# Local attention with values product in channel-major form, tile by tile in turn, and weights divided on GpSimd; state-space stage with rests and root kept in PSUM

## The chip, the cores and the metric

The kernel runs on one core of a Trainium2 chip. A core has TensorE (called PE in the profile; its weight loads are the row PEld), VectorE (DVE), ScalarE (ACT), GpSimd (POOL), SyncE (SP, which issues DMAs here) and 16 DMA engines. The engines run side by side and meet through semaphores. SBUF is the on-chip memory; PSUM holds TensorE's results in eight banks of 128 partitions by 512 fp32 words. The metric is the device time of one execution in microseconds, less is better.

## The reference, cut to what matters

Eight sequences of 256 tokens with 128 channels pass through an attention layer, a hard-routed feed-forward layer, a state-space layer and six layers of windowed local attention, each with a gated feed-forward layer. The change touches the last two of these four stages.

```python
# state-space stage: the norm in front of it, and the low-rank projection
h = _layernorm(x) * (1 + ca) + sa
x_dbl = xs @ W_x                    # 64 columns for dt, 16 for B, 16 for C
# local attention, 6 layers, 16 heads of 64 channels, windows of 32 tokens
q, k = rotary(l2norm(q)*qs), rotary(l2norm(k)*ksc)
sim = einsum('bhwie,bhwje->bhwij', bq, bk2) * QK_SCALE   # bk2: own window and the one before
attn = softmax(where(mask, -max, sim))
out = einsum('bhwij,bhwje->bhwie', attn, bv2)
x = out.reshape(b, n, INNER) @ Wo + x
# feed-forward layer
xn = (x - mu) / sqrt(var + 1e-05) * g + bln
x = (a * gelu(gate)) @ W2 + b2 + x                        # a, gate = split(xn @ W1 + b1)
```

## The kernel before, in words

The program has four stages: attention, routed layer, state-space (`mamba1`) and local attention (`local1`). The data that the change touches is fp32; an fp32 matmul appears in the trace as two passes, a transpose as one.

`local1` is a software pipeline. A step is one sequence (of 8) of one layer (of 6), so there are 48 steps, and the loop runs 50 iterations. In iteration `it` three parts run together: FRONT works on step `it`, MID on step m = it-1, LATE on step n = it-2. Each engine has a hand-written order (`body` in each engine's block) of the same pieces, and each engine works strictly through its own. The table `order` gives every PSUM result ("job") a bank; `jobs.filled` and `jobs.taken` are semaphore waits for "written" and "copied out", and `jobs.free` is the wait before a bank is written again.

The names of the jobs: Z are projections of tokens to queries and keys (`project`, L2052; first digit is the half of the tokens t, second is query 0 or key 1), T their transposes (`turn`, L2063), S scores (`scores`, a mask matmul at L2073 and 64 small ones at L2080), V values of the tokens (`project_values`, L2093), P transposed softmax weights (`turn_weights`, L2105), O the product of weights and values (`values`, L2120), OT its transposes (`turn_outputs`, L2135), WO the output projection (`outputs`, L2146), mean and var the norm, F the hidden layer (`hidden`, L2172), OUT2 its second matmul (`hidden_out`, L2181).

In `values` the stationary operand is a 64 by 32 piece of the transposed weights `pT` and the moving operand 64 columns of values. The result O has tokens on partitions. VectorE divides it by the row sums on the way out (`by_sum`, L2496, into `Ot`), TensorE turns `Ot` (OT), and ScalarE copies that to `oT` (`take_outputs`, L2298), which WO reads. GpSimd has `take_tokens` (L2395), `rotary_sum` (L2402) and `unit` (L2412). VectorE has `less_maximum` (scores minus maximum into z), ScalarE `exps` (L2268), VectorE `sums` (row sums and reciprocal).

The values are needed twice, for two window alignments (`Vo`, `Ve`). ScalarE copies V out of PSUM into `Vo` (`take_values`, L2278), signals `V_ready` and `wv_used`, and SyncE then copies `Vo` to `Ve` by four DMAs (`share_values`, L2001 and L2002). SyncE has one order for everything, `layer` in its block, and the weights of the next layer pass through it too:

```python
if b == NB - 1 and not last:
    sp.wait_ge(qk_used, l * NB + NB)
    load_front(there)
    sp.wait_ge(wv_used, l * NB + NB)
    load_values(there)
share_values(l * NB + b)                 # waits for V_ready of this step
if b == 1 and not first:
    ...load_hidden(here)...load_late(here)
    rest_loaded(l)                       # sem_inc(mid_ok), sem_inc(late_ok)
if b == NB - 1 and not last:
    front_loaded(l + 1)                  # sem_inc(front_ok), sem_inc(values_ok)
```

TensorE waits for `front_ok` at the head of the iteration, before Z00, and for `mid_ok` at the head of `outputs` (WO).

`mamba1` is a pipeline over the eight sequences. `root_variance` writes the reciprocal root of the variance to `lrs` in SBUF and VectorE's `by_root` (L1725) multiplies by it. `first_rest` and `second_rest` (L1729, L1734) form what is left of an fp32 number after its bf16 parts, in `rest` in SBUF.

Of the kernel before, what the change touches and what calls it, by code (L numbers as in the profile page):

```python
# [14 lines left out]
NT = T // 128  # L15
# [1357 lines left out]
def mamba1(core):  # L1373
    nc, d = core.nc, core.dram
    NG = NS // 2
    with ExitStack() as ctx:
# [23 lines left out]
        xd_ready, p1_ready, p2_ready, r2_ready, parts_ready, soft_ready, dt_ready = (  # L1400
            S(n, 1) for n in ("xdbl", "part1", "part2", "rest2", "parts", "soft", "dt"))
# [10 lines left out]

        made = lambda b, name: b + part_of[name]
# [13 lines left out]
        with nc.Block() as block:  # L1427
# [158 lines left out]
            def _(act):  # L1586
# [28 lines left out]
                def root_variance(it):  # L1615
                    act.wait_ge(*jobs.filled(it, "var"))
                    nc.scalar.activation(lrs[:, :], jobs.out("var")[:, 0:T], ACT.Ln, bias=core.eps[:, EPS_LN:EPS_LN + 1])\
                        .then_inc(jobs.sem_drained("var"), 1)
                    act.drain()
                    nc.scalar.activation(lrs[:, :], lrs[:, :], ACT.Exp, scale=-0.5).then_inc(scaled.sem, 1)  # L1620
# [20 lines left out]
                def second_part(it, parts):  # L1641
                    act.wait_ge(*jobs.taken(it, "XD"))
                    nc.scalar.activation(parts[32:64, :], rest[:, :], ACT.Copy).then_inc(p2_ready.sem, 1)

                def third_part(it, parts):
                    act.wait_ge(r2_ready.sem, r2_ready.at(it, 1))
                    nc.scalar.activation(parts[64:96, :], rest[:, :], ACT.Copy).then_inc(parts_ready.sem, 1)
# [62 lines left out]
            def _(dve):  # L1710
# [12 lines left out]
                def by_root(it):  # L1723
                    dve.wait_ge(scaled.sem, scaled.at(it, 1))
                    nc.vector.tensor_tensor(cent[:, :], cent[:, :], lrs[:, :], ALU.mult).then_inc(hm_ready.sem, 1)  # L1725

                def first_rest(it, parts):
                    dve.wait_ge(p1_ready.sem, p1_ready.at(it, 1))
                    nc.vector.tensor_tensor(rest[:, :], jobs.out("XD")[DTR:96, 0:T], parts[0:32, :], ALU.subtract)\  # L1729
                        .then_inc(jobs.sem_drained("XD"), 1)  # L1730

                def second_rest(it, parts):
                    dve.wait_ge(p2_ready.sem, p2_ready.at(it, 1))
                    nc.vector.tensor_tensor(rest[:, :], rest[:, :], parts[32:64, :], ALU.subtract).then_inc(r2_ready.sem, 1)  # L1734
# [91 lines left out]
def local1(core):  # L1826
# [3 lines left out]
    with ExitStack() as ctx:  # L1830
# [22 lines left out]
        Ot = sb("Ot3", [128, NT, H1, E1])  # L1853
# [21 lines left out]
        with nc.Block() as block:  # L1875
# [29 lines left out]
            def _(dve):  # L1905
# [4 lines left out]
                with dve.Fori(0, NB) as b:  # L1910
# [26 lines left out]
        e_ready = S("exps", NT)  # L1937
# [4 lines left out]
        order = (two(FRONT, "Z00", 7, 2) + two(MID, "T11", 5, 3) + [(LATE, "WO", 4)] + two(MID, "T10", 1, 6)  # L1942
                 + two(FRONT, "Z01", 0, 5) + [(LATE, "mean", 4)] + two(MID, "P0", 7, 2) + two(MID, "S1", 6, 1)
                 + two(FRONT, "T00", 3, 7) + [(LATE, "var", 2)] + two(FRONT, "Z11", 0, 4) + two(MID, "O0", 3, 5)
                 + [(FRONT, "V0", 2), (FRONT, "V1", 7)] + two(FRONT, "Z10", 1, 6) + two(MID, "P1", 2, 3)
                 + [(LATE, "F0", 7), (LATE, "F1", 0), (LATE, "F2", 5)] + two(MID, "O1", 4, 2)
                 + [(FRONT, "V2", 3), (FRONT, "V3", 6)] + two(FRONT, "T01", 7, 1) + [(LATE, "OUT2", 5)]
                 + two(MID, "OT1", 3, 2) + two(FRONT, "S0", 0, 6) + two(MID, "OT0", 1, 4))
# [14 lines left out]
        with nc.Block() as block:  # L1963
# [74 lines left out]
            def _(pe):  # L2038
# [27 lines left out]
                def scores(it, t):  # L2066

                    for j in range(2):
                        pe.wait_ge(*jobs.taken(it, f"T{t}{1 - t}.{j}"))
# [38 lines left out]
                def values(it, m, t):  # L2108
# [6 lines left out]
                    for i in range(H1):  # L2115
                        j, h = i % 2, i // 2
                        p, n = 64 * j, f"O{t}.{j}"
                        for w in range(4):
                            V = Ve if w % 2 == 0 else Vo
# [3 lines left out]
                        if i >= H1 - 2:  # L2123
                            last.then_inc(jobs.sem_filled(n), 1)

                def turn_outputs(it, t):

                    for j in range(2):
                        pe.wait_ge(*jobs.taken(it, f"O{t}.{j}"))
                    for j in range(2):  # L2130
                        n = f"OT{t}.{j}"
                        pe.wait_ge(*jobs.free(it, n))
                        for i in range(4):
                            pair = Ot[:, t, 8 * j + 2 * i:8 * j + 2 * i + 2, :].rearrange("p s e -> p (s e)")
                            last = nc.tensor.transpose(jobs.out(n)[:, i * 128:(i + 1) * 128], pair, core.ident[:, :])  # L2135
                        last.then_inc(jobs.sem_filled(n), 1)

                def outputs(it, n):

                    pe.wait_ge(mid_ok, n + 1)  # L2140
                    for t in range(NT):
                        for j in range(2):
                            pe.wait_ge(*jobs.taken(it - 1, f"OT{t}.{j}"))
# [41 lines left out]
                def body(it, front, mid, late):  # L2185
# [13 lines left out]
                    do(mid, pair("T11"), turn, m, 1, 1)  # L2199
# [540 lines left out]
```

## Time and profile before

| what | value |
|---|---|
| time, median of 3 runs | 2901.34 us (2898.34 to 2903.61) |
| the profiled execution | 2920.77 us, its span 2919.0 us |
| PE busy | 2534.2 us (87%) |
| DVE busy | 2114.7 us (72%) |
| ACT busy | 1789.1 us (61%) |
| POOL busy | 1299.7 us (45%) |
| local attention, about | 1250 to 2880 us of the span |
| state-space, about | 850 to 1204 us |

Busy time is a sum over instructions that may overlap on PE, so what a piece costs TensorE is better read from start to start in the timeline. The profile's chain of waits that ended last shows only the last copies and says nothing here, so the stages are read by windows and by the timeline of one iteration. An idle time in brackets stands before the instruction of that row, and the name behind the arrow is what ended it.

### The profile page before, as it was taken

The page shows a single profiled execution, that of the slowest core. Times are in us where ns is not written, and L with a number is a line of the kernel's source. Part 1 is how long each engine was busy: PE and PEld are TensorE (multiplying, and loading weights), DVE is VectorE, ACT ScalarE, POOL GpSimd, SP SyncE. Part 2 cuts the span into 40 slices and gives each one's busy share as a digit, 9 for nine tenths or more (in the row PEclk, how much of TensorE's full clock was granted, in tenths as well). Part 3 has the DMA queues.
Part 4 walks back from the last instruction along what each step waited for, and adds up shares of the span by engine and source line. Part 5 has one row for each costly group of instructions (what it writes and reads, how often), then busy time and mean ns, then how long its engine had stood idle before and what let it go on. Part 6 is the DMA issues. An engine that isn't in the chain of part 4 may idle for free. (4 is left out here: it accounts for less than half of the span.)

```text
span 2919.0 us, 95512 instructions
## 1 busy us (share of the span) xinstructions
PE 2534.2 (87%) x35932; PEld 1738.5 (60%) x35932; DVE 2114.7 (72%) x3264; ACT 1789.1 (61%) x3671; POOL 1299.7 (45%) x966
## 2 busy tenths in 40 slices
PE   7999758885737777569999999999999999999995
PEld 4777446664523334226777677776777767776774
DVE  5888543213217999558888888888888888888883
ACT  4666513332216677346777777777777777777772
POOL 2444232223023444335555555555555555555550
PEclk9999968987858999779999999999999999999997
DMA  9000016860420000011121112111211111121110
GB/s 331 24 0 0 4 41 175 227 168 22 130 65 1 0 0 0 16 50 27 31 53 40 25 25 59 40 25 25 54 45 25 47 40 29 34 54 33 25 36 18
DMA packets 124766, 149.22 MB, mean 51 GB/s; under 512 B 12016, under 2 KB 111536, under 8 KB 120240
## 3 DMA queue, kind: packets, MB, share of 16 engines
q1 hardware_dynamic: 120592, 139.81, 18.0%
q0 software_dynamic: 4096, 8.40, 1.0%
q8 instruction: 45, 0.74, 0.1%
q14 instruction: 33, 0.27, 0.0%
HBM read 76.86 MB, written 27.26 MB: 36 GB/s over the span
## 5 line engine op out<-in xcount | busy, mean ns | idle before, releaser
L2402 POOL TENSOR_TENSOR c<-a,bq 128x1024 f32<-128x1024 f32 x192 | 454.2, 2366 | 380.5 <-DVE bq L2458 380.5
L2412 POOL TENSOR_TENSOR qn<-c,ss 128x1024 f32<-128x1024 f32 x192 | 378.4, 1971 | 28.5 <-issue 7.2
L2052 PE MATMUL ps<-wqk,xs 128*128 128x512 f32 x768 | 373.0, 609 | 12.2 <-POOL xs L2395 8.7
L2237 ACT ACTIVATE sq<-ps 128x512 f32<-128x512 f32 x384 | 223.4, 594 | 93.3 <-PE ps L2052 93.2
L2457 DVE TENSOR_TENSOR a<-ps,tab 128x512 f32<-128x512 f32 x384 | 262.8, 684 | 24.1 <-ACT sq L2237 13.7
L2458 DVE TENSOR_TENSOR bq<-ps,tab 128x512 f32<-128x512 f32 x384 | 261.6, 681 | 0.0
L2465 DVE TENSOR_REDUCE ss<-sq 128x16 f32<-128x1024 f32 x192 | 232.4, 1211 | 14.5 <-issue 14.5
L1458 POOL TENSOR_TENSOR hC<-hs,Cs 128x1024 f32<-128x1024 f32 x64 | 151.9, 2376 | 199.9 <-ACT Cs L1609 104.5
L2052 PEld LDWEIGHTS ps<-wqk,xs 128*128 128x128 f32 x768 | 135.9, 192 | 150.1 <-issue 138.4
L2063 PEld LDWEIGHTS ps<-ident,qn 128*128 128x128 f32 x1536 | 172.2, 141 | 79.4 <-issue 66.9
L2063 PE MATMUL ps<-ident,qn 128*128 128x128 f32 x1536 | 204.8, 276 | 3.2 <-PEq L2045 3.2
L2093 PE MATMUL ps<-wv,xs 128*64 128x512 f32 x768 | 187.7, 609 | 3.2 <-PEq L2045 3.2
L2146 PE MATMUL ps<-oT,wo 128*128 128x256 f32 x768 | 176.8, 384 | 1.8 <-PEq L2045 1.8
L2254 ACT ACTIVATE qT<-ps 128x512 f32<-128x512 f32 x192 | 104.3, 595 | 95.8 <-PE ps L2063 95.8
L2120 PEld LDWEIGHTS ps<-Ve,pT 64*32 64x32 f32 x6144 | 125.7, 105 | 56.0 <-issue 56.0
L1757 DVE TENSOR_TENSOR_SCAN hs<-dA,ps 128x1024 f32<-128x1024 f32 x64 | 146.4, 2287 | 14.6 <-issue 13.9
L1532 PE MATMUL ps<-hC,ident 128*128 128x512 f32 x256 | 139.8, 685 | 19.3 <-POOL hC L1458 19.1
L2146 PEld LDWEIGHTS ps<-oT,wo 128*128 128x128 f32 x768 | 144.3, 193 | 20.2 <-issue 2.0
L2278 ACT ACTIVATE Vo<-ps 128x512 f32<-128x512 f32 x192 | 114.8, 598 | 62.9 <-PE ps L2093 58.6
L2080 PEld LDWEIGHTS ps<-kT,qT 64*32 64x32 f32 x12288 | 127.3, 105 | 43.3 <-issue 43.3
L2496 DVE TENSOR_TENSOR Ot<-ps,sm 128x512 f32<-128x512 f32 x192 | 123.7, 686 | 31.6 <-PE ps L2120 21.0
L2080 PE MATMUL ps<-kT,qT 64*32 64x64 f32 x12288 | 143.0, 225 | 2.5 <-issue 2.5
(309 smaller groups left out, 5882.3 us busy)
## 6 DMA issues: line engine op xcount, KB each, us to landing
Ve<-Vo SPq DMA_DIRECT2D x96, 256.0 KB, 4.3
Ve<-Vo SPq DMA_DIRECT2D x96, 192.0 KB, 4.4
win_rows<-rows_q SPq DMA_DIRECT2D x24, 256.0 KB
outs_q<-win_out SPq DMA_DIRECT2D x24, 256.0 KB
wqk<-in_wqkv SPq DMA_DIRECT2D x6, 1024.0 KB, 5.0
leaves<-in_f_w SPq DMA_DIRECT2D x9, 576.0 KB
leaves<-in_q_w SPq DMA_DIRECT2D x1, 4608.0 KB, 18.8
leaves<-in_k_w SPq DMA_DIRECT2D x1, 4608.0 KB, 22.3
```

What stands on the lines that cost most here:

```text
L1458: nc.gpsimd.tensor_tensor(four(hC), four(hs), spread(Cs[:, s, :], 2), ALU.mult).then_inc(hC_ready.sem, 1)
L2052: nc.tensor.matmul(jobs.out(n), xs[:, t * 128:(t + 1) * 128], wqk[:, (2 * y + s) * 512:(2 * y + s + 1) * 512], start=True, stop=True).then ...
L2063: last = nc.tensor.transpose(jobs.out(n)[:, i * 128:(i + 1) * 128], src, core.ident[:, :])
L2080: last = nc.tensor.matmul(jobs.out(n)[w * W:(w + 1) * W, m * 64:(m + 1) * 64], qT[p:p + 64, t, m, w * W:(w + 1) * W], kT[p:p + 64, even:od ...
L2093: last = nc.tensor.matmul(jobs.out(n)[p:p + 64, :], xs[:, g * 64:(g + 1) * 64], wv[:, p * 8:p * 8 + 512], start=True, stop=True, tile_posi ...
L2146: last = nc.tensor.matmul(jobs.out("WO")[:, 0:T], wo[:, i, :], oT[:, i, :], start=(i == 0), stop=(i == H1 // 2 - 1))
L2237: nc.scalar.activation(sq[:, y, :, s, :], heads_view(jobs.out(n)), ACT.Square).then_inc(sq_ready.sem, 1)
L2402: nc.gpsimd.tensor_tensor(f(c), f(a), f(bq), ALU.add).then_inc(c_ready.sem, 1)
L2412: nc.gpsimd.tensor_tensor(qn[:, t, y, :, :, :].rearrange("p h s e -> p h (s e)"), c[:, y, :, :, :].rearrange("p h s e -> p h (s e)"), spre ...
L2457: nc.vector.tensor_tensor(a[:, y, :, s, :], Zs, spread(table(0, s), H1), ALU.mult)
L2458: nc.vector.tensor_tensor(bq[:, y, :, 1 - s, :], Zs, spread(table(1, 1 - s), H1), ALU.mult)\
L2465: nc.vector.tensor_reduce(ss[:, y, :], sq[:, y, :, :, :].rearrange("p h s e -> p h (s e)"), axis=AX.X, op=ALU.add)\
```

## The change

In `local1`, `values` swaps the operands. The stationary operand is now a 64 by 64 piece of values, the moving one 32 columns of `pT`, and the result O has channels on partitions, as WO wants them. The order of the small matmuls runs over four heads before the next window, so that the four 64 by 64 tiles of the array come in turn. OT, `turn_outputs`, `Ot` and VectorE's `by_sum` are gone, and ScalarE copies O straight to `oT`. The rows of `Wo` are laid out anew on the host to fit. The division moves ahead of the transposition of the weights: GpSimd's new `by_sum` multiplies z by the reciprocal sums, and P waits for it. The orders of TensorE, ScalarE, VectorE and GpSimd and the table of banks are written anew. SyncE's code is the same.

```diff
                     for i in range(H1):
-                        for w in range(4):
-                            last = nc.tensor.matmul(jobs.out(n)[w * W:(w + 1) * W, h * 64:(h + 1) * 64],
-                                                    pT[p:p + 64, t, h, w * W:(w + 1) * W], V[p:p + 64, 2 * t + w // 2, h, :],
-                                                    start=True, stop=True, tile_position=(p, w * W))
+                    for i, w in [(i, w) for m4 in range(0, H1, 4) for w in range(4) for i in range(m4, m4 + 4)]:
+                        half, at = 64 * (h % 2), (h // 2) * 128 + w * W
+                        last = nc.tensor.matmul(jobs.out(n)[half:half + 64, at:at + W], V[p:p + 64, 2 * t + w // 2, h, :],
+                                                pT[p:p + 64, t, h, w * W:(w + 1) * W], start=True, stop=True, tile_position=(p, half))
...
+                def by_sum(m, t):
+                    pool.wait_ge(sums_ready.sem, sums_ready.at(m, t + 1))
+                    nc.gpsimd.tensor_tensor(z[:, t, :, :], z[:, t, :, :], spread(sm[:, t, :], 2 * W, 2), ALU.mult).then_inc(weights_ready.sem, 1)
...
                 def turn_weights(it, m, t):
-                    pe.wait_ge(e_ready.sem, e_ready.at(m, t + 1))
+                    pe.wait_ge(weights_ready.sem, weights_ready.at(m, t + 1))
...
-                    do(mid, pair("OT1"), turn_outputs, 1)
                     do(front, pair("S0"), scores, 0)
-                    do(mid, pair("OT0"), turn_outputs, 0)
```

ScalarE's `take_values(it, 1)` with its signals `V_ready` and `wv_used` moves to the last place of the body, behind the copy of O1, the exponentials of S0 and a root:

```diff
                     if late:
                         gelus(it, n)
-                    if front:
-                        take_values(it, 1)
+                    if mid:
+                        take_outputs(it, m, 1)
+                    if front:
+                        exps(it, 0, it)
+                        roots(it, 1, 0)
+                        take_values(it, 1)
                         act.drain()
                         act.sem_inc(V_ready.sem, 1)
                         act.sem_inc(wv_used, 1)
-                        turned(it, 0, 1)
-                        roots(it, 1, 1)
```

In `mamba1` the reciprocal root and the rests stay in PSUM, in the free halves of the banks of "var" and "XD". `by_root` gets a drain before its signal, and ScalarE's `third_part` too.

```diff
+        rest, lrs = jobs.out("XD")[DTR:96, T:2 * T], jobs.out("var")[:, T:2 * T]
...
-                    nc.vector.tensor_tensor(cent[:, :], cent[:, :], lrs[:, :], ALU.mult).then_inc(hm_ready.sem, 1)
+                    nc.vector.tensor_tensor(cent[:, :], lrs, cent[:, :], ALU.mult).then_inc(jobs.sem_drained("var"), 1)
+                    dve.drain()
+                    dve.sem_inc(hm_ready.sem, 1)
```

How the orders move. First TensorE at the end of the loop's body, before: V2 and V3 (L2093), T01 (L2063), OUT2 (L2181), OT1 (L2135), the mask and scores of S0 (L2073, L2080), OT0.

```order
1361 L2093 MATMUL ps<-wv,xs 64x512 x2
1362 L2091 REGISTER_ALU
1363 L2093 MATMUL ps<-wv,xs 64x512 x2
1364 L2057 REGISTER_ALU
1365 L2063 MATMUL ps<-ident,qn 128x128 x4
1366 L2060 REGISTER_ALU
1367 L2063 MATMUL ps<-ident,qn 128x128 x4
1368 L2178 REGISTER_ALU
1369 L2181 MATMUL ps<-hid,w 128x256
...
1374 L2135 MATMUL ps<-ident,Ot 128x128 x8
```

The same place after the change: V2 and V3 (L2094), O1 (L2121, sixteen such rows), OUT2 (L2169), end of the loop.

```order
1160 L2094 MATMUL ps<-wv,xs 64x512 x2
1161 L2092 REGISTER_ALU
1162 L2094 MATMUL ps<-wv,xs 64x512 x2
1163 L2114 REGISTER_ALU x2
1164 L2121 MATMUL ps<-pT,Ve 64x32 x4
1165 L2121 MATMUL ps<-pT,Vo 64x32 x4
...
1182 L2169 MATMUL ps<-hid,w 128x256 x3
1183 L1959 REGISTER_ALU
1184 L1959 COMPARE_AND_BRANCH
```

The transposes of `Ot` are gone, S0 and T01 stand earlier, and only OUT2 is left between O1 and the next iteration's Z00.

Second, ScalarE at the end of its body, before: the last gelu (L2329), the copies of V2 and V3 (L2278), T01 (L2260), a root.

```order
642 L2329 ACTIVATE gl<-ps,par 85x256
643 L2331 ACT_TABLE_LOAD
644 L2273 REGISTER_ALU
645 L2277 REGISTER_ALU
646 L2278 ACTIVATE Vo<-ps 128x512
647 L2277 REGISTER_ALU
648 L2278 ACTIVATE Vo<-ps 128x512
649 L2260 ACTIVATE kT<-ps 128x2x128 x2
```

After: the copy of O1 (L2284), exponentials (L2254), a root (L2229, L2231), and the copies of V2 and V3 (L2264) last.

```order
640 L2317 ACT_TABLE_LOAD
641 L2283 REGISTER_ALU
642 L2284 ACTIVATE oT<-ps 128x4x128
643 L2283 REGISTER_ALU
644 L2284 ACTIVATE oT<-ps 128x4x128
645 L2254 ACTIVATE z<-z 128x1024
646 L2228 REGISTER_ALU
647 L2229 ACTIVATE ss<-ss,eps 128x16
648 L2231 ACTIVATE ss<-ss,eps 128x16
649 L2263 REGISTER_ALU
650 L2264 ACTIVATE Vo<-ps 128x512
```

The copies of V2 and V3, after which SyncE may go on, have moved behind four ScalarE pieces, the first of which needs O1.

## Rows read from the trace of the kernel before

**Rows 1.** Windows: stretch, then busy time per engine, granted clock, DMA share, GB/s.
```profile
850.00:1204.00 354.00, 249.69 (x796) 130.32 (x796) 290.29 (x274) 223.60 (x475) 152.06 (x66) 0.87 0.03 8
1250.00:2880.00 1630.00, 1593.05 (x31170) 1114.31 (x31170) 1379.61 (x2182) 1204.25 (x2444) 893.75 (x624) 0.99 0.15 37
```
**Rows 2.** Timeline of POOL, two iterations' first instruction: start, duration, instruction.
```profile
2016.51 0.40 POOL L2395 COPY xs<-Y 128x256 f32 x1 [4.66 <-PE ps L2093]
...
2049.49 0.40 POOL L2395 COPY xs<-Y 128x256 f32 x1 [4.66 <-PE ps L2093]
```
**Rows 3.** Timeline of PE over one iteration's turn.
```profile
2017.06 1.46 PE L2181 MATMUL ps<-hid,w 128*128 128x256 f32 x6
2018.36 1.04 PE L2135 MATMUL ps<-ident,Ot 128*128 128x128 f32 x8
2019.23 0.59 PE L2073 MATMUL ps<-wmask_b,ident_b 128*128 128x512 bf16 x2
...
2021.17 1.09 PE L2135 MATMUL ps<-ident,Ot 128*128 128x128 f32 x8
2022.10 1.88 PE L2052 MATMUL ps<-wqk,xs 128*128 128x512 f32 x4
2023.82 1.04 PE L2063 MATMUL ps<-ident,qn 128*128 128x128 f32 x8
...
2037.16 0.24 PE L2120 MATMUL ps<-Ve,pT 64*32 64x64 f32 x1
...
2038.43 0.22 PE L2120 MATMUL ps<-Vo,pT 64*32 64x64 f32 x1
2038.58 1.94 PE L2093 MATMUL ps<-wv,xs 128*64 128x512 f32 x8
```
**Rows 4.** Groups by line of PE's weight loads, 1300 to 2880 us: busy, mean ns.
```profile
L2120 PEld LDWEIGHTS ps<-Ve,pT 64*32 64x32 f32 x6144 | 125.7, 105 | 56.0 <-issue 56.0
L2093 PEld LDWEIGHTS ps<-wv,xs 128*64 128x64 f32 x752 | 45.6, 136 | 62.3 <-issue 53.7
```
**Rows 5.** Timeline of the weight loads of the first V job.
```profile
2038.57 0.20 PEld L2093 LDWEIGHTS ps<-wv,xs 128*64 128x64 f32 x4
```
**Rows 6.** Groups by line on DVE and POOL, 1300 to 2880 us.
```profile
L2412 POOL TENSOR_TENSOR qn<-c,ss 128x1024 f32<-128x1024 f32 x188 | 370.8, 1972 | 28.0 <-issue 7.2
L2496 DVE TENSOR_TENSOR Ot<-ps,sm 128x512 f32<-128x512 f32 x192 | 123.7, 686 | 31.6 <-PE ps L2120 21.0 <-issue 10.5
```
**Rows 7.** Timeline of ACT: at the end of a layer, and the exponentials elsewhere.
```profile
1521.53 0.60 ACT L2278 ACTIVATE Vo<-ps 128x512 f32<-128x512 f32 x1 [0.26 <-PE ps L2093]
...
1526.40 0.31 ACT L2243 ACTIVATE ss<-ss,eps 128x16 f32<-128x16 f32 x1 [0.94 <-DVE ss L2465]
1526.77 0.31 ACT L2245 ACTIVATE ss<-ss,eps 128x16 f32<-128x16 f32 x1
1527.18 1.08 ACT L2298 ACTIVATE oT<-ps 128x512 f32<-128x512 f32 x2
...
2038.06 1.05 ACT L2268 ACTIVATE z<-z 128x1024 f32<-128x1024 f32 x1
```
**Rows 8.** Timeline of SP's DMA issues, b = 7 of a layer, then b = 1.
```profile
1522.26 0.33 SPq L1973 DMA_DIRECT2D wv<-in_wqkv  x1
...
1524.63 1.00 SPq L2002 DMA_DIRECT2D Ve<-Vo  x1
...
1588.16 0.52 SPq L2001 DMA_DIRECT2D Ve<-Vo  x1
...
1593.23 0.36 SPq L1983 DMA_DIRECT2D par<-in_params  x1
```
**Rows 9.** Timeline of PE around an idle stretch, and a window in it.
```profile
1326.12 0.31 PE L2080 MATMUL ps<-kT,qT 64*32 64x64 f32 x6 [2.48 <-issue]
...
1327.29 3.33 PE L2052 MATMUL ps<-wqk,xs 128*128 128x512 f32 x4
...
1328.00:1329.00 1.00, 1.00 (x3) 0.48 (x2) 0.53 (x1) 0.18 (x2) 0.00 (x0) 0.50 0.09 16
```

More of the change, by code:

```diff
@@ L1936, in local1 @@
         c_ready, qn_ready = S("c", NQ, NQ), S("qn", NQ, NQ)
-        e_ready = S("exps", NT)
+        e_ready, sums_ready, weights_ready = S("exps", NT), S("sums", NT), S("weights", NT)
         squared, scaled, xm_ready, xn_ready, gl_ready = S("squared", 1), S("scaled", 1), S("xm", 1), S("xn", 1), S("gl", FC)
         two = lambda part, n, b0, b1: [(part, n + ".0", b0), (part, n + ".1", b1)]
[L1942 to L1948, printed above, removed]
+        order = (two(FRONT, "Z00", 0, 7) + [(LATE, "WO", 4)] + two(MID, "T10", 1, 0) + two(FRONT, "Z01", 5, 3) + two(MID, "T11", 0, 4)
+                 + two(MID, "P0", 7, 1) + [(LATE, "mean", 6)] + two(MID, "S1", 0, 5) + two(FRONT, "Z11", 2, 7) + [(LATE, "var", 4)]
+                 + two(MID, "O0", 6, 3) + two(FRONT, "T00", 1, 0) + [(FRONT, "V0", 6), (FRONT, "V1", 4)] + two(FRONT, "T01", 5, 7)
+                 + two(FRONT, "Z10", 3, 2) + two(FRONT, "S0", 5, 0) + two(MID, "P1", 7, 1)
+                 + [(LATE, "F0", 6), (LATE, "F1", 3), (LATE, "F2", 4), (FRONT, "V2", 1), (FRONT, "V3", 2)] + two(MID, "O1", 5, 0)
+                 + [(LATE, "OUT2", 3)])
         jobs = Jobs(core.banks, [(n, b, 1) for _, n, b in order], N + 2)
@@ L2068, in scores @@
                     for j in range(2):
-                        pe.wait_ge(*jobs.taken(it, f"T{t}{1 - t}.{j}"))
+                        pe.wait_ge(*jobs.taken(it, f"T{t}1.{j}"))
                     for j in range(2):
@@ L2114, in values @@
                     pe.sem_inc(pe_steps, 1)
[L2115 removed]
+                    for i, w in [(i, w) for m4 in range(0, H1, 4) for w in range(4) for i in range(m4, m4 + 4)]:
                         j, h = i % 2, i // 2
                         p, n = 64 * j, f"O{t}.{j}"
[L2118 to L2136 removed]
+                        V = Ve if w % 2 == 0 else Vo
+                        half, at = 64 * (h % 2), (h // 2) * 128 + w * W
+                        last = nc.tensor.matmul(jobs.out(n)[half:half + 64, at:at + W], V[p:p + 64, 2 * t + w // 2, h, :],
+                                                pT[p:p + 64, t, h, w * W:(w + 1) * W], start=True, stop=True, tile_position=(p, half))
+                        if i >= H1 - 2 and w == 3:
+                            last.then_inc(jobs.sem_filled(n), 1)
                 def outputs(it, n):
@@ L2142, in outputs @@
                         for j in range(2):
-                            pe.wait_ge(*jobs.taken(it - 1, f"OT{t}.{j}"))
+                            pe.wait_ge(*jobs.taken(it - 1, f"O{t}.{j}"))
                     pe.wait_ge(*jobs.free(it, "WO"))
@@ L2367, in body @@
                     if front:
[L2368 to L2370 removed]
+                        roots(it, 1, 1)
                     if mid:
@@ L2485, in sums @@
                     dve.drain()
[L2486 to L2499 removed]
+                    nc.vector.reciprocal(sm[:, t, :], sm[:, t, :]).then_inc(sums_ready.sem, 1)
                 def center(it, n):
@@ L2578, in body @@
                     if front:
-                        square_sums(it, 1, 0)
+                        sums(it, 0)
                 dve.sem_inc(late_Y.sem, late_Y.credit)
```

140 lines of the change are left out of this document (61 added, 79 removed).

## The prediction

> **What bounds the kernel now.** I read the windows by stage first. Local attention takes the stretch from 1250 to 2880 us, and there TensorE is busy 1593 of 1630 us at a granted clock of 0.99, VectorE 1380, ScalarE 1204, GpSimd 894 [rows 1]. TensorE's own instructions are the bound, and nearly nothing is waited for. The first GpSimd instruction of an iteration comes 32.98 us after that of the one before [rows 2], and 49.4 such periods fill the 1630 us. So a microsecond off TensorE's work in an iteration is worth 48 us, and so is one that is put on it, as long as the others keep up. Work taken from VectorE is worth nothing by itself. The timeline of TensorE then gives each piece its price from its start to the start of the next piece [rows 3], which is better than its busy time because matmuls overlap. The state-space stage is 354 us, with VectorE busy 290 [rows 1].
>
> **Transposes of the output, removed.** OT1 runs from 2018.36 to 2019.23, OT0 from 2021.17 to 2022.10 [rows 3]: 0.87 + 0.93 = 1.80 us less in each iteration.
>
> **Values, operands swapped.** O0 starts at 2037.16 and the next piece at 2038.58 [rows 3], 1.42 us for 64 small matmuls, that is 128 passes on eight tiles of 64 by 32. After the change there are as many passes, on four tiles of 64 by 64, each with 32 columns to stream instead of 64 and 64 columns of weights to load instead of 32. The four projections of Z00 stream 4 x 512 columns in 1.72 us (2022.10 to 2023.82) [rows 3], 0.84 ns a column, so a pass streams for 54 ns before and 27 ns after. A load of 32 columns lasts 105 ns, one of 64 lasts 136 ns [rows 4], 31 ns for 32 more columns. The four loads of V0, two on each of two tiles, end 0.20 us after the first began [rows 5]; without the 0.136 of the last and 7 ns between the tiles this is 57 ns between two loads on one tile. So the load is now longer than the stream and sets the pace: 32 passes on each tile x 57 ns = 1.82, and 0.15 at the end (last pass at 2038.43, next piece at 2038.58 [rows 3]), 1.97 us. That is 0.55 more for each of the two jobs, 1.10 in an iteration. The bounds: loads and streams of one tile never side by side, 32 x (57 + 27) = 2.69, with the end 2.84; streams alone, 32 x 30 ns = 0.96, with the end 1.11. I take the middle case, since the transposes show a load hidden behind a stream of the same rows of the array: eight in 0.87 us, 109 ns each [rows 3], where streaming 128 columns takes 107 alone. The new order of jobs also changes the shape of the tiles once more in an iteration, at most the 0.15 above; I take 0.10. TensorE's iteration gets 1.80 - 1.10 - 0.10 = 0.60 us shorter, 48 x 0.60 = 29 us.
>
> **Division on GpSimd.** VectorE loses four instructions of 686 ns an iteration [rows 6], worth nothing beside TensorE. GpSimd gains two of about 1.97 us (L2412 has their shape [rows 6]). It is busy 894/49.4 = 18.1 us of 32.98 now [rows 1] and would be at 22.0. P0 and P1 now wait for sums and the division, and behind P stand all later pieces of TensorE. For half 0: the root that GpSimd's last `unit` waits for is there 1.6 us after Z00 is due (the 2.7 of `V_ready` below less its two copies), `unit` takes some 2.4 and the division 2.0, which makes 6.0. P0 stands behind Z00 and Z01 (1.72 each), two transposes (0.88 each) and WO (16 passes of 256 columns at 0.84 ns, 3.44), at 8.6. For half 1 a similar count leaves about 1 us. I cost it at 0. If this cover failed by half a microsecond in each iteration it would be 24 us.
>
> **The signal behind the copies of V2 and V3, moved.** This step costs most. SyncE goes on to `share_values`, and at the end of a layer to `front_loaded`, only after `V_ready`. Before, the last copy of V ended at 1521.53 + 0.60 = 1522.13, SyncE's issues at 1524.63 + 1.00 = 1525.63, and OT0 was only copied from 1527.18 [rows 7, 8], so `front_ok` came before Z00 needed it. Now ScalarE copies V last. After O1 it has the copy of O1, 1.09 us, the exponentials, 1.05, a root, 0.31 + 0.31 and gaps, 0.75, and two copies, 1.10 as the pair of the same shape [rows 7], together 3.99. TensorE has only OUT2 after O1, 1.30 us (2017.06 to 2018.36 [rows 3]). So `V_ready` comes 2.7 us after Z00 is due. In a usual iteration nobody minds: O0 needs the shared values some 14 us later. But at the end of a layer Z00 needs `front_ok`, which stands behind the load of wv and four more issues in SyncE's queue: 1525.63 - 1522.13 = 3.50 us, and 0.1 to TensorE. Z00 waits 2.7 + 3.6 = 6.3 us, and all of TensorE behind it. Two iterations later it comes again: `mid_ok` is given after four shares, w1, w2 and the parameters, from 1588.16 to 1593.23 + 0.36 = 1593.59, 5.43 us [rows 8], with 0.13 before and 0.1 after. WO now stands second on TensorE and is due 1.72 us after Z00, where T11 stood between them before. It waits 2.7 + 5.66 - 1.72 = 6.6 us. There are five changes of layer: 5 x 12.9 = 65 us. I bound each wait by 4.5 and 8 us, 45 to 80 in all, as ScalarE may be earlier or later by 1 to 2 us.
>
> **The clock after such a wait.** After TensorE stood 2.48 us, the four projections from 1327.29 took 3.33 us at a granted clock of 0.50, the lower level of 1.2 GHz, against 1.88 at the full one [rows 9, 3]. A wait of 6 us should end so too: 10 x 1.45 = 15 us, with 0 and 30 as bounds.
>
> **State-space.** PSUM instead of SBUF for small operands and two drains, on eight sequences. From -2 to +4 us by 0.5 us a sequence; I take 0, with the end of local attention, where the last division and OT leave the chain, at -1 to -3, in it.
>
> **Sum.** -29 + 65 + 15 = +51 us. On the profiled execution this is 2920.8 + 51 = 2972, on the median 2901.3 + 51 = 2952.
>
> **Rivals.**
> Loads not hidden: a value job takes 2.84 us, 0.87 more than forecast, 1.74 an iteration, 84 us: 3036. For it speaks that on the eight tiles of 64 by 32, with 16 passes each, 16 x (26 + 54 ns) = 1.28 us is what comes out if nothing overlaps within a tile (26 ns being the 57 less 31), close to the 1.27 from the first pass to the last; against it the transposes above, and V, whose loads hide. The Trainium skill, "TensorE: Matmul & The Clock Gate", Part 3, The mechanism, says that a weight load overlaps a matmul in flight only where the row groups differ. By that rule the sum would be this rival's; the transposes of this trace do not bear it out.
>
> The short stream decides, and the kernel is faster: if two loads of one tile overlap, a value job takes 1.11 us, an iteration is 1.80 + 0.62 - 0.10 = 2.3 us shorter, 111 us, against 80 for waits and clock: 2870. It decides from 1.67 us an iteration on (80/48), which needs a job of at most 1.43. For it: eight tiles take 10 ns a pass. Against: the 57 ns between two loads of one tile. The Trainium skill, "TensorEngine Tiling (Array Packing)", Performance Considerations, says that a matmul of one column takes as long as one of sixty. By that rule halving the stream would give little, and a job would stay near 1.4; no row here has so short an fp32 stream.
>
> The waits do not come: if ScalarE had the V copies done in time, or SyncE's issues were shorter, only the 29 us of TensorE stay: 2872. Against it stands the order of ScalarE's instructions, which does not bend.
>
> New waits in each iteration, for the division, the copies of T or of O1 just before Z00: 0.5 us x 48 = 24 more, 2976. Several of these are within half a microsecond in my layout.
>
> **How the numbers follow.** Forecast 0.62, with its own range 2930 to 2975; loads not hidden 0.12; short stream 0.10; no waits 0.07; new waits 0.09. The predicted time is 2952. The range from 2870 to 3005 leaves out the first rival and the lower half of the second. A measurement of this kernel can tell about 0.2%, 6 us, from no change. Faster by more: no waits and half of the short stream, 0.12. Within 0.2%: the other half, about 0.06 with a corner of no waits. Slower: the rest, 0.82.
>
> **What would show it.** In the changed profile: an iteration of about 32.4 us away from the layers' ends; value jobs of 1.97 us from start to start; no OT; before Z00 at five places TensorE idle for 6 us until SyncE's signal, and again before WO two iterations later; the low clock right after; the last V copy after OUT2. Wrong it would be if an iteration took 33 us or more, or if TensorE did not stand at the ends of the layers.

## The result: 1.7% slower, and where the profile after shows it

| | before | after |
|---|---|---|
| median of 4 runs | 2902.48 us (2898.34 to 2903.70) | 2956.02 us (2951.31 to 2956.91) |
| ratio, 95% interval | | 1.0167 (1.0148 to 1.0186) |
| profiled execution, span | 2920.77, 2919.0 us | 2956.91, 2955.1 us |

The forecast was 2952 us. The changed kernel is 48.5 us slower by its ratio; the two medians lie 53.5 us apart, and the interval of the ratio covers 43 to 54 us. The one profiled execution of before was some 18 us above its median, so the profiled spans differ by only 36 us: before spent 14.9 us more ahead of its first state-space scan (889.1 against 874.2 us), and these are left out of the ledger.

First the busy times of the changed kernel (page, first part). PE and DVE do less, GpSimd does more, and still the kernel is slower: busy times do not answer the question.

```profile
PE 2525.4 (85%) x35164; PEld 1719.4 (58%) x35164; DVE 2007.8 (68%) x3072; ACT 1761.7 (60%) x3671; POOL 1467.3 (50%) x1062
```

The usual iteration is shorter. Here is the first GpSimd instruction of two iterations (timeline: start, duration, instruction):

```profile
1672.63 0.40 POOL L2379 COPY xs<-Y 128x256 f32 x1
1705.22 0.40 POOL L2379 COPY xs<-Y 128x256 f32 x1
```

It is 32.59 us where before had 32.97 [rows 2], 0.38 less. The two value jobs of one iteration follow in TensorE's timeline (each O job is 16 rows of 8 passes):

```profile
1672.12 0.32 PE L2121 MATMUL ps<-pT,Ve 64*64 64x32 f32 x8
...
1672.26 0.30 PE L2121 MATMUL ps<-pT,Vo 64*64 64x32 f32 x8
1672.38 0.30 PE L2121 MATMUL ps<-pT,Ve 64*64 64x32 f32 x8
...
1674.12 1.57 PE L2169 MATMUL ps<-hid,w 128*128 128x256 f32 x6
1675.53 1.88 PE L2053 MATMUL ps<-wqk,xs 128*128 128x512 f32 x4
...
1689.23 0.59 PE L2149 MATMUL ps<-lsq,mean_w 128*128 128x256 f32 x2
1689.75 0.32 PE L2121 MATMUL ps<-pT,Ve 64*64 64x32 f32 x8
...
1691.75 1.09 PE L2064 MATMUL ps<-ident,qn 128*128 128x128 f32 x8
1692.78 0.65 PE L2094 MATMUL ps<-wv,xs 128*64 128x512 f32 x2
```

From the first pass of O1 to OUT2 it is 2.00 us, from O0 to T00 also 2.00 (forecast 1.97, before 1.42 [rows 3]). No OT stands here. OUT2 takes 1.41 us to the next piece, 1.30 before [rows 3].

Ten iterations are long, two at each of the five layer changes: 40.1 to 41.1 us where `front_ok` is late and 40.9 to 42.6 where `mid_ok` is. Together they have 85.7 us more than ten usual ones. TensorE's waits in local attention (what waited, on what: total, times, longest):

```profile
PE ps L2134 <- SPq L1994: 33.6, 5, 6.8
PE ps L2053 <- SPq L1988: 30.1, 5, 6.1
```

The first is WO behind `mid_ok`, the second Z00 behind `front_ok`. Neither is there before. The chain at one layer change reads as forecast. ScalarE, the last copies of V:

```profile
1493.72 1.09 ACT L2284 ACTIVATE oT<-ps 128x512 f32<-128x512 f32 x2 [1.93 <-PE ps L2121]
...
1496.24 1.08 ACT L2264 ACTIVATE Vo<-ps 128x512 f32<-128x512 f32 x2
```

SyncE, which goes on only then:

```profile
1497.46 0.33 SPq L1974 DMA_DIRECT2D wv<-in_wqkv  x1
...
1499.85 0.92 SPq L2003 DMA_DIRECT2D Ve<-Vo  x1
```

and TensorE, at this change and two iterations later:

```profile
1500.96 3.46 PE L2053 MATMUL ps<-wqk,xs 128*128 128x512 f32 x4 [5.80 <-SPq L1988]
1504.26 3.62 PE L2134 MATMUL ps<-oT,wo 128*128 128x256 f32 x16
...
1576.37 6.72 PE L2134 MATMUL ps<-oT,wo 128*128 128x256 f32 x16 [6.77 <-SPq L1994]
1582.93 1.04 PE L2064 MATMUL ps<-ident,qn 128*128 128x128 f32 x8
```

Z00 was due at 1500.96 - 5.80 = 1495.16. The copies of V ended 2.16 us later (1497.32), SyncE's issues 3.45 after that (1500.77), and 0.19 more passed to TensorE. The projections of Z00 then took 3.30 us to the start of WO, against 1.71 in another iteration (1675.53 to 1677.24), and behind WO's own wait WO took 6.56 (1576.37 to 1582.93), where it otherwise takes 3.45 (1504.26 to 1507.71). Windows around and after these waits (stretch, busy time of PE, PEld, DVE, ACT and POOL, granted clock, DMA share, GB/s):

```profile
1494.00:1495.00 1.00, 1.00 (x6) 0.68 (x4) 0.00 (x0) 1.00 (x3) 0.00 (x0) 1.00 0.00 0
...
1577.00:1580.00 3.00, 3.00 (x9) 2.37 (x8) 0.00 (x0) 0.00 (x0) 0.00 (x0) 0.50 0.12 34
```

The clock is at its full level of 2.4 GHz before the wait and at 0.50, 1.2 GHz, behind it. These two waits do not stand for all ten. At the next layer change the same pieces show other lengths:

```profile
1779.57 3.77 PE L2053 MATMUL ps<-wqk,xs 128*128 128x512 f32 x4 [6.12 <-SPq L1988]
1783.14 3.98 PE L2134 MATMUL ps<-oT,wo 128*128 128x256 f32 x16
...
1855.55 5.38 PE L2134 MATMUL ps<-oT,wo 128*128 128x256 f32 x16 [6.71 <-SPq L1994]
1860.78 1.04 PE L2064 MATMUL ps<-ident,qn 128*128 128x128 f32 x8
```

From start to start Z00 takes 3.57 us here, the WO behind it 3.82 (to 1786.96), and WO behind its own wait 5.23.

The state-space stage, from its first to its last scan, went from 308.6 to 298.7 us, which was not forecast. Groups by line on VectorE of that stage (busy, mean ns of one), before:

```profile
L1734 DVE TENSOR_TENSOR rest<-rest,parts 32x256 f32<-32x256 f32 x7 | 14.4, 2060 | 0.2
L1725 DVE TENSOR_TENSOR cent<-cent,lrs 128x256 f32<-128x256 f32 x7 | 10.1, 1445 | 1.8 <-ACT lrs L1620 1.8
L1743 DVE TENSOR_TENSOR du<-dt,xs 128x512 f32<-128x512 f32 x7 | 7.9, 1135 | 0.6
L1729 DVE TENSOR_TENSOR rest<-ps,parts 32x256 f32<-32x256 f32 x7 | 2.9, 419 | 0.2
```

and the same steps after:

```profile
L1737 DVE TENSOR_TENSOR ps<-ps,parts 32x256 f32<-32x256 f32 x7 | 3.1, 436 | 2.6 <-ACT parts L1643 2.3
L1727 DVE TENSOR_TENSOR cent<-ps,cent 128x256 f32<-128x256 f32 x7 | 2.9, 417 | 1.9 <-ACT ps L1620 1.8
L1746 DVE TENSOR_TENSOR du<-dt,xs 128x512 f32<-128x512 f32 x7 | 4.8, 692 | 0.6
```

The second rest fell from 2060 to 436 ns, the product with the root from 1445 to 417. `du` fell too, from 1135 to 692, though its operands did not move. The last section says why.

The ledger in the profiled spans, in us: the 47 periods from one iteration's start to the next's, 0.39 shorter each, -18.4 (before has five of 33.06 among its own), ten long ones +85.7, the filling of the pipeline -1.4, its end -4.6 (from the last iteration's first instruction 110.9 before, 106.3 after), the state-space stage -9.9, and the way between the two stages -0.4. That is +51.0, where the ratio says +48.5.

### The profile page after: what moved, and what is told of

The parts are those of the page before. It is cut to its first block and busy times, and to the rows that moved or that the text cites. A ratio compares the mean times of both kernels' runs of the same rounds, so it can differ in the third digit from the quotient of the medians.

```text
span 2955.1 us, 93444 instructions
## 1 busy us (share of the span) xinstructions
PE 2525.4 (85%) x35164; PEld 1719.4 (58%) x35164; DVE 2007.8 (68%) x3072; ACT 1761.7 (60%) x3671; POOL 1467.3 (50%) x1062
## 5 line engine op out<-in xcount | busy, mean ns | idle before, releaser
L2396 POOL TENSOR_TENSOR qn<-c,ss 128x1024 f32<-128x1024 f32 x192 | 365.4, 1903 | 28.4 <-issue 3.4
L2404 POOL TENSOR_TENSOR z<-z,sm 128x1024 f32<-128x1024 f32 x96 | 182.7, 1903 | 117.0 <-DVE sm L2479 106.3
L2134 PE MATMUL ps<-oT,wo 128*128 128x256 f32 x768 | 185.7, 397 | 35.7 <-SPq L1994 33.6
L2134 PEld LDWEIGHTS ps<-oT,wo 128*128 128x128 f32 x768 | 154.2, 202 | 82.7 <-issue 62.2
L2121 PEld LDWEIGHTS ps<-pT,Ve 64*64 64x64 f32 x6144 | 163.9, 134 | 57.0 <-issue 57.0
L2094 PE MATMUL ps<-wv,xs 128*64 128x512 f32 x768 | 189.2, 614 | 2.6 <-PEq L2046 2.6
L2284 ACT ACTIVATE oT<-ps 128x512 f32<-128x512 f32 x192 | 104.2, 595 | 146.0 <-PE ps L2121 146.0
L2121 PE MATMUL ps<-pT,Ve 64*64 64x32 f32 x6144 | 187.6, 220 | 2.0 <-PEq L2046 1.8
L2121 PE MATMUL ps<-pT,Vo 64*64 64x32 f32 x6144 | 185.6, 219 | 0.0
L2121 PEld LDWEIGHTS ps<-pT,Vo 64*64 64x64 f32 x6144 | 164.4, 135 | 0.0
L2394 POOL TENSOR_SCALAR ss<-ss 128x16 f32<-128x16 f32 x192 | 47.2, 246 | 234.3 <-ACT ss L2231 214.5
```

The lines of the kernel that those rows point to most:

```text
L2094: last = nc.tensor.matmul(jobs.out(n)[p:p + 64, :], xs[:, g * 64:(g + 1) * 64], wv[:, p * 8:p * 8 + 512], start=True, stop=True, tile_posi ...
L2121: last = nc.tensor.matmul(jobs.out(n)[half:half + 64, at:at + W], V[p:p + 64, 2 * t + w // 2, h, :], pT[p:p + 64, t, h, w * W:(w + 1) * W] ...
L2134: last = nc.tensor.matmul(jobs.out("WO")[:, 0:T], wo[:, i, :], oT[:, i, :], start=(i == 0), stop=(i == H1 // 2 - 1))
L2396: nc.gpsimd.tensor_tensor(qn[:, t, y, :, :, :].rearrange("p h s e -> p h (s e)"), c[:, y, :, :, :].rearrange("p h s e -> p h (s e)"), spre ...
L2404: nc.gpsimd.tensor_tensor(z[:, t, :, :], z[:, t, :, :], spread(sm[:, t, :], 2 * W, 2), ALU.mult).then_inc(weights_ready.sem, 1)
```

## The experiments

All times are of the one core. The chips of these runs gave the kernel before medians of 2905 to 2914 us, so each is read by its ratio to before and not by its microseconds. e5, e6 and e7 are one run each and are read from their traces.

### e1_early_signals: the signals taken out from behind the copies

The loads stay in SyncE's queue at their places, but `front_ok` and `mid_ok` are each given once their own weights have landed, ahead of `share_values`, and no longer behind it. `values_ok` and `late_ok` stay behind it.

```diff
     load_mid(here)
+    sp.wait_ge(wo_loaded, l * 16 + 16)
+    sp.sem_inc(mid_ok, NB)
...
     load_front(there)
+    sp.wait_ge(qk_loaded, l * 16 + 32)
+    sp.sem_inc(front_ok, NB)
     sp.wait_ge(wv_used, l * NB + NB)
     load_values(there)
 share_values(l * NB + b)
```

> The changed kernel, but SyncE gives front_ok as soon as wqk has landed and mid_ok as soon as wo has landed, ahead of the shares of the values and the other loads. Theory (the two waits at each change of layer come from signals that stand in SyncE's queue behind V_ready): TensorE no longer stands before Z00 and WO there, every iteration takes 32.6 us, and the 5 x 17 us that these iterations take beyond that are gone: 2956 - 86 = 2870 us. Rival (the weights themselves land late, or the late copy of V blocks something else): the waits stay, 2950 us or more. Rival (the waits go and the clock's loss with them only in part): 2885 us.

Measured: ratio 0.9888 (0.9870 to 0.9907), median 2881.23 us. Every iteration from the fifth on is 32.58 to 32.60 us, none is long, and no wait for SyncE is left on TensorE. At the place of the layer change:

```profile
1500.29 1.57 PE L2175 MATMUL ps<-hid,w 128*128 128x256 f32 x6
1501.70 1.88 PE L2059 MATMUL ps<-wqk,xs 128*128 128x512 f32 x4
```

Z00 comes 1.41 us after OUT2 with no idle time, at the full clock (1.88 us). The position of two signals is thus worth 0.0279 of 2902, 81 us (expected 86), and without it the change is a gain. This version beats both kernels.

### e3_front_only: only `front_ok` early

```diff
     load_front(there)
+    sp.wait_ge(qk_loaded, l * 16 + 32)
+    sp.sem_inc(front_ok, NB)
```

> The changed kernel with front_ok alone given early. Theory: the five long iterations before Z00 (7.6 to 8.5 us over the usual 32.6) become usual, the five before WO (8.3 to 10.0 over) stay: 2956 - 40 = 2916 us. Rival (one late signal moves only into the other, since V_ready is the same): no gain, 2956.

Measured: ratio 1.0021 (1.0008 to 1.0034). The waits of Z00 are gone, and five iterations are long, 41.5 us each, with this wait:

```profile
PE ps L2137 <- SPq L1994: 33.5, 5, 6.7
```

The two signals divide the price into 42 us (front) and 39 us (mid), and they are independent: WO's wait two iterations later is as long (33.5 us in five) without the first.

### e2_copies_first: the copies of V2 and V3 ahead of the root and the exponentials

```diff
                     if mid:
                         take_outputs(it, m, 1)
-                    if front:
-                        exps(it, 0, it)
-                        roots(it, 1, 0)
                     if front:
                         take_values(it, 1)
                         ...
+                        roots(it, 1, 0)
+                        exps(it, 0, it)
```

> The changed kernel, but ScalarE copies V2 and V3 right after O1, ahead of the root and the exponentials, so V_ready comes 1.8 us earlier. Theory (wait = distance of V_ready from when Z00 and WO are due, plus SyncE's issues): the waits shrink from 6.1 and 6.8 to 4.3 and 5.0 us, ten times 1.8 = 18 us less, the iterations elsewhere stay at 32.6: 2938 us. Rival (the wait is the landing of weights): no change, 2956. Rival (the exponentials, now 1.1 us later, hold up sums, division and P0): each iteration longer by up to 0.5 us, 2960.

Measured: ratio 1.0218 (1.0198 to 1.0238), a miss: slower than the change itself. The waits did shrink, by 1.5 us each where 1.8 were expected, but a new one came, named in 36 of the iterations:

```profile
PE ps L2134 <- SPq L1994: 26.3, 5, 5.3
PE ps L2053 <- SPq L1988: 22.8, 5, 4.7
PE ps L2064 <- DVE bq L2451: 15.9, 36, 0.7
```

The exponentials now start 2.97 us after the copy of O1, behind two copies and a root, where they started 0.97 us after it. VectorE's sums wait for them, and the rotation that stands behind the sums delays the transposes behind WO, which take 1.53 us to the next piece for 0.87: 33.24 us an iteration, 0.65 more. VectorE at that place:

```profile
1682.79 1.22 DVE L2477 TENSOR_REDUCE sm<-z 128x16 f32<-128x1024 f32 x1 [1.57 <-ACT z L2254]
```

Of the 2.00 us, about 1.35 were covered (an estimate, 2.00 less 0.65). The rest costs more over the usual iterations than the shorter waits give back at ten. The signal was to be moved on SyncE, not on ScalarE.

### e5_long_stream and e6_half_load: does the load set the pace of a value job?

e5 streams 64 columns a pass instead of 32; e6 loads 32 instead of 64 (its ScalarE copy of O is a Relu in place of a Copy).

```diff
# e5
-                        half, at = 64 * (h % 2), (h // 2) * 128 + w * W
-                        last = nc.tensor.matmul(jobs.out(n)[half:half + 64, at:at + W], V[p:p + 64, 2 * t + w // 2, h, :],
-                                                pT[p:p + 64, t, h, w * W:(w + 1) * W], start=True, stop=True, tile_position=(p, half))
+                        c = min(w, 2) * W
+                        half, at = 64 * (h % 2), (h // 2) * 128 + c
+                        last = nc.tensor.matmul(jobs.out(n)[half:half + 64, at:at + 2 * W], V[p:p + 64, 2 * t + w // 2, h, :],
+                                                pT[p:p + 64, t, h, c:c + 2 * W], start=True, stop=True, tile_position=(p, half))
# e6
-                        last = nc.tensor.matmul(jobs.out(n)[half:half + 64, at:at + W], V[p:p + 64, 2 * t + w // 2, h, :],
+                        last = nc.tensor.matmul(jobs.out(n)[half:half + 32, at:at + W], V[p:p + 64, 2 * t + w // 2, h, 0:32],
                                                 pT[p:p + 64, t, h, w * W:(w + 1) * W], start=True, stop=True, tile_position=(p, half))
```

> The changed kernel, but each small matmul of the value product streams 64 columns of pT instead of 32 (the results overlap, so the output is another one). Everything else, the number of loads (64 columns each) and their order are the same. My theory (the load sets the pace, 57 ns between two loads on one tile, and the stream of 54 ns lies beside it): a value job stays at about 2.0 us from start to start, the iteration at 32.6 us, the time within 1% of the changed kernel's 2956. Rival (load and stream of one tile follow one another): a job grows by 32 passes x 27 ns = 0.86 us to about 2.85, the iteration to about 34.3 us and the time by some 80 us. If the stream alone decided (two loads overlap), the job would also grow, by up to 0.86.

> The changed kernel, but the stationary operand of the value product is 64 by 32 instead of 64 by 64: it leaves out the upper 32 of each head's 64 channels (the copy of O clips what is left in the bank with a Relu instead of a plain copy). The streams stay at 32 columns, the number of passes too. My theory (loads set the pace, 57 ns for 64 columns, about 26 to 41 ns for 32): a value job falls from 2.0 to 1.0 to 1.5 us and the iteration from 32.6 to about 31.0 to 31.6 us, the time by 50 to 75 us. Rival (something else than the load, such as a fixed cost of a pass, sets 62 ns a pass on a tile): the job stays at 2.0 us and the iteration at 32.6.

In e5 the results of neighbouring windows overlap, and e6 leaves out half of the channels, so both give another output. Measured, e5: 2957.55 us, iteration 32.64 us, a job of 2.03 us:

```profile
1717.79 0.34 PE L2122 MATMUL ps<-pT,Ve 64*64 64x64 f32 x8
1717.96 0.30 PE L2122 MATMUL ps<-pT,Vo 64*64 64x64 f32 x8
...
1719.82 1.09 PE L2064 MATMUL ps<-ident,qn 128*128 128x128 f32 x8
```

Twice the stream costs 0.03 us a job. e6: 2890.20 us, iteration 31.15 us, jobs of 1.32 and 1.22 us:

```profile
1720.34 0.27 PE L2121 MATMUL ps<-pT,Ve 64*32 64x32 f32 x8
1720.42 0.24 PE L2121 MATMUL ps<-pT,Vo 64*32 64x32 f32 x8
1720.48 0.24 PE L2121 MATMUL ps<-pT,Ve 64*32 64x32 f32 x8
```

Eight passes, two on each tile, come every 0.117 us with 64 columns to load and every 0.065 to 0.07 with 32. That is 58 and some 33 ns between two loads on one tile. A stream of up to 54 ns is hidden beside a load of 64 columns, and both rivals for this (load and stream in series, a fixed cost of a pass) are out: the columns of the stationary operand set the pace. That it is their load, and not for instance the writing of the result, whose partitions e6 halves too, is argued from the loads' own rows, 58 ns apart, and not separated by a run.

### e7_tiles_in_a_row: four matmuls on one tile, then the next tile

```diff
-for i, w in [(i, w) for m4 in range(0, H1, 4) for w in range(4) for i in range(m4, m4 + 4)]:
+for i, w in [(i, w) for i in range(H1) for w in range(4)]:
```

> The changed kernel with the small matmuls of the value product in the old order: four windows of one head, all on the same 64 by 64 tile, one behind the other, then the next head, instead of the four tiles in turn. Loads and streams are the same in number and size. 
Measured (one run): 3192.31 us, a job of 4.48 us, an iteration of 37.55.

```profile
1709.70 0.30 PE L2121 MATMUL ps<-pT,Ve 64*64 64x32 f32 x4
...
1709.96 0.30 PE L2121 MATMUL ps<-pT,Ve 64*64 64x32 f32 x4
```

A new head starts every 0.26 us, and four tiles no longer work at once. Eight passes 58 ns apart would take 0.46 us; the first passes of the next head run beside the last of this one, hence 4.48 and not the 7.4 us of a full series (128 x 58 ns). "Tiles in turn" is worth 2 x 2.48 us an iteration. Without it the change would be far slower than it is.

### e4_sbuf_state and e8_before_psum_state: the state-space part by itself

e4 is the changed kernel with that part undone, e8 the kernel before with that part alone. The edit (here as e8 has it):

```diff
+        rest, lrs = jobs.out("XD")[DTR:96, T:2 * T], jobs.out("var")[:, T:2 * T]
...
-  nc.vector.tensor_tensor(rest[:, :], rest[:, :], parts[32:64, :], ALU.subtract)
+  nc.vector.tensor_tensor(rest, rest, parts[32:64, :], ALU.subtract)
```

> The changed kernel with the state-space stage as before: rests and root in SBUF. Theory (a VectorE tensor_tensor with both inputs in SBUF stands until GpSimd's instruction of 2.35 us is over; one with an input in PSUM does not): the second rest lasts 2.1 us again instead of 0.44 and the product with the root 1.4 instead of 0.42, the stage is 10 us longer: 2966 us. Rival (the stage differed for another reason, such as the clock in that run): the stage stays at 299 us from first scan to last, 2956 us.

> The kernel before, with the state-space part of the change alone: the rests and the reciprocal root of the variance in PSUM, with the two drains. In the changed kernel the stage took 298.7 us and with the old form 312.1. If the gain is the one of the state-space stage alone and is kept to the end: the stage falls from 308.6 to about 298.5 us and the time by 10 us, a ratio of 0.9965. Rival (the gain in the changed kernel came from elsewhere or is given back in what follows): ratio 0.999 to 1.001. The prediction had 0, with -2 to +4 us.

Measured: e4 ratio 1.0207 (1.0189 to 1.0224), its stage 312.1 us; e8 ratio 0.9969 (0.9955 to 0.9983), its stage 300.8 us. In e4 the long instructions are back (group of the product with the root; the second rest again has 2060 ns):

```profile
L1725 DVE TENSOR_TENSOR cent<-cent,lrs 128x256 f32<-128x256 f32 x7 | 10.0, 1430 | 1.8 <-ACT lrs L1620 1.8
```

Both ways the part is worth 9 to 12 us (0.0031 and 0.0040 of 2902). The second is a difference of two ratios, each known to about 0.0018, so it is rough; the stage itself, in the traces, is 13.4 us longer in e4 and 7.8 shorter in e8.

### e9_vector_division: the division back on VectorE

```diff
-    nc.gpsimd.tensor_tensor(z[:, t, :, :], z[:, t, :, :], spread(sm[:, t, :], 2 * W, 2), ALU.mult).then_inc(weights_ready.sem, 1)
...
     nc.vector.reciprocal(sm[:, t, :], sm[:, t, :])
+    dve.drain()
+    nc.vector.tensor_tensor(z[:, t, :, :], z[:, t, :, :], spread(sm[:, t, :], 2 * W, 2), ALU.mult).then_inc(weights_ready.sem, 1)
```

> The changed kernel with the early signals of e1_early_signals, and the division of the weights by the sums taken from GpSimd and given to VectorE, right behind its reciprocal (with a drain between). It tests the term "division on GpSimd: 0". If GpSimd's division is well covered, it cannot be beaten by more than a measurement can tell: ratio 0.989 as e1_early_signals, iteration 32.6 us. VectorE has 1270 us busy of 1640 in local attention and gains 96 instructions of 1.1 to 2 us (SBUF to SBUF, 1024 elements), 105 to 190 us, so 85% or more busy; if that shifts the copies and rotations TensorE waits for, the iteration grows by 0.5 to 2 us and the time by 25 to 100 us, ratio 0.998 to 1.023. I hold the second for likelier, by 0.5 us an iteration. If instead the iteration falls below 32.5 us, GpSimd's division was on the path after all.

Measured: ratio 0.9992 (0.9977 to 1.0007), an iteration of 33.31 us, 0.72 more than e1. All of it stands at the transposes behind WO, 1.59 us to the next piece for 0.87 in e1. TensorE waits there in 46 of the iterations:

```profile
PE ps L2070 <- DVE bq L2456: 22.5, 46, 0.5
```

while e1, with the division on GpSimd, has no such line. Behind it stand VectorE's new instructions:

```profile
L2486 DVE TENSOR_TENSOR z<-z,sm 128x1024 f32<-128x1024 f32 x93 | 171.7, 1846 | 6.9
```

They are long because GpSimd is at work beside them, as in the last section. One runs from 1418.30 to 1420.24, 1.94 us, and ends 1.09 us behind a GpSimd `c<-a,bq` (1416.79 to 1419.15); two early ones took 1.23 us in all. So the 0.72 us hold the added work and this standing, and no run separates the two. On GpSimd the division costs nothing in a usual iteration, on VectorE 0.72 us.

## Why the prediction was right, step by step

**Sign, size and cause** were right: forecast 2952 us, measured 2956, by the mechanism named, and e1 shows that without the late signals the sign turns. Several terms were off, and partly cancelled.

**Transposes of the output, -1.80 an iteration.** Right; no L2135 is left.

**Value job, 1.97 us.** Measured 2.00. Its reason stood on two rows of before, the load of [rows 4] and the pitch of 57 ns [rows 5]. e5, e6 and e7 bear it out: 58 ns between two loads of one tile, whatever the stream up to 54 ns. The rival "loads not hidden" (2.84 us) is out. The Trainium skill, "TensorE: Matmul & The Clock Gate", Part 3, The mechanism, says in its list of what overlaps that a load does so only where the row groups differ, though its first paragraph also allows a load into a background buffer; doubling the stream in e5 would by the list's rule have lengthened the job, and it did not. The rival "short stream decides" (1.11 us) is out too, by the 2.00 (its 30 ns a pass had no row behind it; the forecast's own streams give 27).

**Change of the tiles' shape, +0.10.** Too small; with the two value jobs at +1.17 for the forecast's 1.10, this step made the iteration's gain 0.38 and not 0.60 us. Where a job of 64 by 64 tiles stands next to one of 128 by 128, the neighbours take longer from start to start: OUT2 1.41 for 1.30, T00 1.03 for 0.93, var 0.52 for 0.43. Over all pieces of one iteration, OUT2 has 0.11 more, the four transposes 0.09, the two P 0.06, var 0.09 and the four projections 0.09 less: before, it was a projection that stood in front of O0 and paid (1.81 for 1.72). That is +0.26, and -1.80 + 1.17 + 0.26 = -0.37, near the -0.38 measured. That the shape is the cause is argued from these rows, not shown by a run; e6, with 64 by 32 tiles, has the same lengths on the same pieces (OUT2 1.40, T00 1.02, var 0.52).

**Division on GpSimd, 0.** Right in the steady state: TensorE's waits in e1 name it once, in the filling of the pipeline. e9 adds that the choice of engine matters.

**Waits at the layer changes, +65.** Measured 63.7: Z00 6.0 us on average (forecast 6.3), WO 6.7 (6.6). The parts for Z00 were 2.16 (forecast 2.7) for ScalarE and 3.64 (3.6) for SyncE and the way to TensorE. e1, e2 and e3 show the cause: the waits vanish when the signal moves, shrink by 1.5 us when V is copied two pieces earlier, and go one by one.

**Clock after a wait, +15.** Too small. The ten long iterations have 85.7 - 63.7 = 22.0 us beyond the idle time. The forecast took 1.45 us from one case [rows 9] for both kinds of wait. Behind the first wait that nearly holds: in three cases Z00 takes 3.25 to 3.33 us for 1.71 and WO behind it its normal 3.45, 1.6 more; in the other two Z00 takes 3.57 and WO 3.80 to 3.82, 2.2 more. Behind the second wait WO itself is the first piece, twice as long as Z00, and it takes 6.56, 5.23, 6.53, 5.21 and 4.95 us for 3.45: 3.1, 1.8, 3.1, 1.8 and 1.5 more. All ten make 20.4, and about 1.6 is how the profile counts idle time (0.16 at each wait, by which a piece otherwise overlaps the one before). The price of a clock that fell is not a constant: it depends on where in the pieces behind the wait the clock comes back, and a long first piece can lose more of it.

**State-space, 0 with -2 to +4.** Wrong: the stage gained 9.9 us, outside the bounds. The step that failed was to price the edit by its drains and accesses, and not to look up the VectorE lines of that stage: L1734 with a mean of 2060 ns beside L1729 of the same shape at 419 stood in the trace of before.

**End of local attention, -1 to -3.** Measured -4.6 from the last iteration's start to the end.

In sum the forecast had -29 + 65 + 15 + 0 = +51, and the trace has -18.4 + 63.7 + 22.0 - 9.9 - 6.4 (the pipeline's two ends and the way between the stages) = +51.0. That 2952 came so near is partly luck: terms that were too kind to the kernel (11 for the iterations, 7 for the clock) met terms that were too hard on it (10 for the state-space stage, 6 for the ends, 1 for the waits). None of the rivals came true. The fourth, new waits in each iteration, is what e2 and e9 run into: 0.65 and 0.72 us an iteration.

## What to carry to other kernels

When a signal moves in one engine's order, follow every queue that waits for it to its end: here ScalarE's last copies held SyncE, and SyncE's queue held signals that had nothing to do with those copies. Give a "weights loaded" signal as soon as those weights have landed, not behind unrelated issues of the same queue: here that was worth 81 us. For many small matmuls look at the load first: doubling the stream cost 0.03 us a job of 2.00, halving the load took a third off, and taking the tiles in turn more than half. Before moving an operand or a division, look up the lines of that stage whose mean is far above that of others of their shape.

## What the runs showed of the hardware that was not expected

A VectorE instruction with both inputs in SBUF does not run beside the GpSimd product of the state-space stage. Before the change, VectorE without GpSimd at work, and with it:

```profile
870.92 0.43 DVE L1725 TENSOR_TENSOR cent<-cent,lrs 128x256 f32<-128x256 f32 x1 [2.77 <-ACT lrs L1620]
...
983.90 1.35 DVE L1725 TENSOR_TENSOR cent<-cent,lrs 128x256 f32<-128x256 f32 x1
...
997.70 2.36 DVE L1734 TENSOR_TENSOR rest<-rest,parts 32x256 f32<-32x256 f32 x1
```

GpSimd at the second and third of these times:

```profile
982.61 2.36 POOL L1458 TENSOR_TENSOR hC<-hs,Cs 128x1024 f32<-128x1024 f32 x1 [2.35 <-DVE hs L1757]
...
997.43 2.35 POOL L1458 TENSOR_TENSOR hC<-hs,Cs 128x1024 f32<-128x1024 f32 x1 [3.23 <-PE ps L1532]
```

GpSimd's instructions end at 984.97 and 999.78, VectorE's at 985.25 and 1000.06: 0.28 us behind them each time. After the change one input of the product with the root is in PSUM. VectorE and, under it, GpSimd:

```profile
966.26 0.41 DVE L1727 TENSOR_TENSOR cent<-ps,cent 128x256 f32<-128x256 f32 x1
```

```profile
964.97 2.35 POOL L1459 TENSOR_TENSOR hC<-hs,Cs 128x1024 f32<-128x1024 f32 x1 [2.37 <-DVE hs L1760]
```

It runs from 966.26 to 966.67, inside GpSimd's 964.97 to 967.32, in 0.41 us. The Trainium skill, "SBUF — State Buffer", section "SBUF: two separate sides", says that of a VectorE instruction with two SBUF inputs and a GpSimd instruction that reads SBUF, the one that starts first takes a pair of ports for its whole length, and that the other one waits. These rows agree with it, and e4 and e8 put its price here at 9 to 12 us. In the last of the eight sequences before, VectorE comes first: its second rest starts at 1158.01 and takes 0.41 us, and the GpSimd product that starts at 1158.12 takes 2.53 in place of 2.35.

`du` has both inputs in SBUF before and after. Before, six of its eight instructions began 1.8 to 1.9 us into GpSimd's product and took 1.21 us; after, most begin some 0.65 us ahead of the next product and take 0.69. So it gained by the new times and not by its operands.
